# Attention: rope steps of the batch two ahead in the first part of a batch, its norm one batch sooner, the residual on GpSimd

## What is computed

```python
q = _layernorm(x); k = v = ctx_1024                      # (16, 256, 256) -> heads of 16
q = q * cos + rotate_half(q) * sin
k = k * cos + rotate_half(k) * sin
scores = einsum('bqhd,bkhd->bhqk', q, k) / 4 + slope[h] * (key - query)
out = einsum('bhqk,bkhd->bqhd', softmax(scores), v)
x = x + tanh(g_xattn[1]) * out
```

## Time and profile before

| | |
|---|---|
| median of 3 runs | 859.51 us (857.71 to 860.60) |
| profiled execution | 860.34 us, its span 858.2 us |
| mean granted TensorE clock | 0.93 |
| TensorE busy | 713.5 us (83% of the span) |
| VectorE busy | 708.5 us (83%) |
| ScalarE busy | 488.0 us (57%) |
| GpSimd busy | 431.1 us (50%) |
| 256 row maxima, VectorE | 166.3 us, 687 ns each |
| chain that ended last | TensorE 33%, VectorE 30%, issue 16%, GpSimd 9%, ScalarE 8% |

### The profile page before, as it was taken

One profiled execution on the slowest core, in us unless ns is written; L12 is line 12 of the kernel. 1 busy time (PEld: TensorE's weight loads), 2 busy tenths in 40 slices (PEclk: granted clock), 3 DMA queues, 4 the chain that ended last, 5 costly groups with the idle time before them and its releaser, 6 DMA issues.

```text
span 858.2 us, 16571 instructions
## 1 busy us (share of the span) xinstructions
PE 713.5 (83%) x5090; PEld 517.0 (60%) x5090; DVE 708.5 (83%) x1230; ACT 488.0 (57%) x939; POOL 431.1 (50%) x331
## 2 busy tenths in 40 slices
PE   2255999999999998779999999999999775777775
PEld 1255888887888877556565555656565333444444
DVE  6867788998889887868898989898888658888885
ACT  3433545445454342337777777777778674555553
POOL 4524565555655545644444554555443526655553
PEclk8576999999999999879999999999999987888898
DMA  8800000000000000010000000000001000100011
GB/s 279 246 3 0 1 1 1 0 0 0 0 0 1 1 1 1 1 50 2 3 2 2 1 1 1 2 1 1 1 1 50 2 1 1 37 25 24 26 37 50
DMA packets 17719, 18.35 MB, mean 21 GB/s; under 512 B 1670, under 2 KB 16912, under 8 KB 17680
## 3 DMA queue, kind: packets, MB, share of 16 engines
q1 hardware_dynamic: 17084, 17.66, 6.4%
q10 hardware_dynamic: 596, 0.20, 0.1%
HBM read 13.39 MB, written 4.19 MB: 20 GB/s over the span
## 4 chain that ended last, share of the span: by engine, by line
PE 33%; DVE 30%; issue 16%; POOL 9%; ACT 8%; DVEq 1%; DMA 1%; POOLq 1%; ACTq 0%; SPq 0%
PE a_ps_t L561 7%; PE a_ps_m L579 6%; DVE maxima L1497 5%; PE a_ps_pv L615 4%; DVE f_ps_small L1582 4%; PE a_ps_s L600 3%; POOL hs L1110 3%; PE ps_o L522 3%; DVE hup L1324 2%; DVE f_hcode L1598 2%; DVE yup L1293 2%; POOL xres L1090 2%; DVE hscale L1318 2%; ACT hmag L866 1%; PE a_ps_pv L623 1%
## 5 line engine op out<-in xcount | busy, mean ns | idle before, releaser
L1497 DVE TENSOR_REDUCE maxima<-a_ps_m 128x2 f32<-128x512 f32 x256 | 166.3, 687 | 35.4 <-PE a_ps_m L579 34.7
L919 ACT ACTIVATE probs<-a_ps_s 128x512 f32<-128x512 f32 x256 | 149.2, 602 | 42.3 <-PE a_ps_s L600 40.1
L579 PE MATMUL a_ps_m<-stack_t 64*128 64x256 f32 x512 | 107.5, 328 | 19.9 <-DVE maxima L1497 16.7
L579 PEld LDWEIGHTS a_ps_m<-stack_t 64*128 64x128 f32 x512 | 68.3, 188 | 78.7 <-DVE maxima L1497 49.5
L600 PE MATMUL a_ps_s<-stack_t 64*128 64x256 f32 x512 | 100.0, 308 | 3.7 <-ACT probs L919 2.9
L1141 POOL TENSOR_TENSOR stack<-roped,stack 128x512 f32<-128x512 f32 x32 | 42.6, 1333 | 116.8 <-DVE stack L1487 115.3
L491 PE MATMUL ps_gu<-w1h,yth 128*128 128x352 f32 x256 | 88.6, 346 | 13.2 <-DVE h L1311 13.2
L522 PE MATMUL ps_o<-w2t,hqt 128*128 128x256 f32 (+1 forms) x384 | 97.9, 390 | 0.2 <-ACT hqt L851 0.2
L615 PE MATMUL a_ps_pv<-probs,v_aug 128*32 128x256 f32 x1024 | 83.0, 396 | 2.9 <-ACT probs L919 2.5
L910 ACT CAST stack_t<-a_ps_t 128x512 fp32r<-128x512 f32 x128 | 70.9, 588 | 24.5 <-PE a_ps_t L561 23.7
L561 PE MATMUL a_ps_t<-idf,stack 128*128 128x128 f32 x512 | 77.2, 294 | 9.0 <-POOL stack L1141 4.6
(11 more groups left out here) (176 smaller groups left out, 1613.3 us busy)
## 6 DMA issues: line engine op xcount, KB each, us to landing
xres<-in_x SPq DMA_DIRECT2D x16, 256.0 KB, 3.2
ctx<-in_ctx SPq DMA_DIRECT2D x16, 256.0 KB, 3.8
out_x<-f_y SPq DMA_DIRECT2D x16, 256.0 KB, 2.1
w1a_raw<-in_w_gate_up SPq DMA_DIRECT2D x1, 1024.0 KB, 6.2
w_raw<-in_w_fc SPq DMA_DIRECT2D x1, 1024.0 KB, 5.7
w_raw<-in_w_proj SPq DMA_DIRECT2D x1, 1024.0 KB, 5.0
w_raw<-in_w_down SPq DMA_DIRECT2D x1, 704.0 KB, 9.3
stack_t<-neg_max_t SPq DMA_DIRECT2D x32, 8.0 KB
```

Source lines behind the costliest of these rows:

```text
L579: ins = nc.tensor.matmul(a_ps_m[:, half, n, :], a_stack_t[b.par][rows, 0, pair, c * P:(c + 1) * P], a_stack_t[b.par][rows, 1, pair, :], st ...
L919: nc.scalar.activation(a_probs[:, u % 8], a_ps_s[:, u % 2], ACT.Exp).then_inc(a_exp, 1)
L1497: nc.vector.tensor_reduce(a_maxima[:, b.par, c, 4 * quad + half:4 * quad + half + 3:2], a_ps_m[:, half], X, ALU.max).then_inc(a_v_max, 1)
```

## The change

- VectorE, body of a batch b: rope sum and cast of k of b+2, then reciprocals and shares of b-1, rope sum and cast of q of b+2, statistics of b+3; rstd/4 and the two norm steps of b+3 come after m=5. The rope sum and the cast of q leave the places after m=5 and m=8.
- GpSimd, body of b: low parts of k and q of b+2, the residual of b-1 (new here), rstd, k products and q products of b+3.
- The gate is taken into v: ScalarE's copy of v becomes a multiplication by the gate. VectorE's gated residual (L1511) goes; GpSimd adds `a_attn` to `xres` (`at_add`).
- New waits: GpSimd for the shares, VectorE's shares for the residual of the batch before, and in the last layer every batch's statistics for that batch's residual, with a semaphore step of VectorE's own behind the wait.
- Before the loop the second batch's norm comes ahead of the maxima, its rope and cast of k after m=3, those of q after m=5, and the third batch's statistics and norm after m=9 and m=12. `ahead` is 3 in place of 2, so four batches at the end are written out on VectorE and GpSimd in place of two.

```diff
-V_QK = ["stats0", "stats1", "aggr0", "aggr1", "var", "rope_k", "k_hi", "rstd4", "norm0", "norm1", "rope_q", "q_hi"]
+V_QK = ["stats0", "stats1", "aggr0", "aggr1", "var", "rstd4", "norm0", "norm1", "rope_k", "k_hi", "rope_q", "q_hi"]
-G_QK = ["k_cos", "k_sin", "rstd", "k_lo", "q_cos", "q_sin", "q_lo"]
+G_QK = ["rstd", "k_cos", "k_sin", "q_cos", "q_sin", "k_lo", "q_lo"]
-V_OUT = ["recip0", "recip1", "share0", "share1", "add"]
+V_OUT = ["recip0", "recip1", "share0", "share1"]
+ATT_AHEAD = 3
...
-                nc.scalar.copy(a_v_aug[:, b.par, :, :, 0:HD].rearrange("p c h d -> p (c h) d"),
-                               tiles(ctx, b).rearrange("p c (h d) -> p (c h) d", d=HD)).then_inc(a_v, 1)
+                nc.scalar.mul(a_v_aug[:, b.par, :, :, 0:HD].rearrange("p c h d -> p (c h) d"),
+                              tiles(ctx, b).rearrange("p c (h d) -> p (c h) d", d=HD), gates[:, 1:2]).then_inc(a_v, 1)
...
+            def at_add(b):
+                pool.wait_ge(a_v_out, upto(V_OUT, b, "share1"))
+                nc.gpsimd.tensor_tensor(tiles(xres, b), tiles(xres, b), a_attn[:, :, :], ALU.add).then_inc(a_g_add, 1)
+
             def at_body(b):
-                nxt2 = b.shifted(2)
+                nxt2, nxt3 = b.shifted(2), b.shifted(3)
                 if nxt2:
-                    at_k_parts(nxt2)
-                    at_rstd(nxt2)
                     at_low_part(nxt2, 1)
-                    at_q_parts(nxt2)
                     at_low_part(nxt2, 0)
-                elif b.shifted(1):
+                if b.shifted(-1):
+                    at_add(b.shifted(-1))
+                if nxt3:
+                    at_rstd(nxt3)
+                    at_k_parts(nxt3)
+                    at_q_parts(nxt3)
+                if b.shifted(1) and not nxt2:
                     w34_round(0)
                     w34_round(1)
...
-            def at_add_attention(b):
+            def at_share(b):
...
+                if b.shifted(-1):
+                    dve.wait_ge(a_g_add, b.shifted(-1).count(1, 1))
...
-                dve.wait_ge(a_v_out, upto(V_OUT, b, "share1"))
-                nc.vector.scalar_tensor_tensor(tiles(xres, b).rearrange("p c d -> p (c d)"), a_attn[:, :, :].rearrange("p c d -> p (c d)"),
-                                               gates[:, 1:2], tiles(xres, b).rearrange("p c d -> p (c d)"),
-                                               ALU.mult, ALU.add).then_inc(a_v_out, 1)
 
             def at_body(b):
-                nxt2 = b.shifted(2)
+                nxt2, nxt3 = b.shifted(2), b.shifted(3)
                 if nxt2:
-                    at_qk_a(nxt2)
                     at_rope(nxt2, 1)
                     at_high_part(nxt2, 1)
-                    at_qk_norm(nxt2)
-                if b.shifted(-1):
-                    at_add_attention(b.shifted(-1))
+                if b.shifted(-1):
+                    at_share(b.shifted(-1))
+                if nxt2:
+                    at_rope(nxt2, 0)
+                    at_high_part(nxt2, 0)
+                if nxt3:
+                    at_qk_a(nxt3)
...
-                    if nxt2 and m == 5:
-                        at_rope(nxt2, 0)
-                    if nxt2 and m == 8:
-                        at_high_part(nxt2, 0)
+                    if nxt3 and m == 5:
+                        at_qk_norm(nxt3)
 
             def ff_input_stats(b):
                 p = b.par
+                dve.wait_ge(a_g_add, b.count(1, 1))
+                dve.sem_inc(f_alone, 1)
...
             at_lay(1)
             at_qk_a(second)
-            at_rope(second, 1)
-            at_high_part(second, 1)
             at_qk_norm(second)
             for m in range(MU):
                 at_row_max(first, m)
+                if m == 3:
+                    at_rope(second, 1)
+                    at_high_part(second, 1)
                 if m == 5:
                     l0_add_ffn(last)
                     at_rope(second, 0)
-                if m == 8:
                     at_high_part(second, 0)
-            over_batches(dve, at_body)
+                if m == 9:
+                    at_qk_a(third)
+                if m == 12:
+                    at_qk_norm(third)
+            over_batches(dve, at_body, ATT_AHEAD)
...
-            at_add_attention(last)
+            at_share(last)
```

More of the change, by code:

```diff
@@ L335, in build_main @@
         a_alone = sem("a_waits_alone")
+        a_g_add = sem("a_residual_ready")
         f_v_ln, f_g_rstd, f_v_shift, f_a_norm = sem("f_v_ln"), sem("f_rstd_ready"), sem("f_shift_ready"), sem("f_normed")
@@ L1227, in _ @@
             l0_hidden_quantised(last)
+            at_rstd(second)
             at_k_parts(second)
-            at_rstd(second)
+            at_q_parts(second)
             at_low_part(second, 1)
-            at_q_parts(second)
             at_low_part(second, 0)
-            over_batches(pool, at_body)
+            at_rstd(third)
+            at_k_parts(third)
+            at_q_parts(third)
+            over_batches(pool, at_body, ATT_AHEAD)
             for b in lead[:3]:
@@ L1239, in _ @@
             ff_input_up(lead[1])
+            at_add(last)
             ff_input_rstd(lead[4])
```

## The result

The changed kernel takes 874.75 us (median of 6 runs, 871.71 to 875.46) against 860.06 us for the kernel before in the same comparison (857.10 to 861.08). The ratio is 1.0168, 95% interval 1.0144 to 1.0193: 14.7 us slower, where the prediction said 861.6 and its range ended at 868. The profiled execution took 872.27 us with a span of 870.5, so its span is 12.3 us above the 858.2 of before. It is one of the faster of the six runs, 2.5 us under their median.

What follows compares the result with a forecast made beforehand. The prediction took TensorE's order (scores, then P times V) to set the pace nearly everywhere in a batch's second part. Its terms, 1.9 + 0 + 0 - 0.4 + 0.7 - 1.3 + 1.2 = +2.1 us, gave 861.6 us; range 855 to 868.

Steps and rivals of the forecast that it cites:

- item 2: After m=5, rstd4 and norm replace the rope sum: m=6 0.25 us later, +1.9 us over 13 batches (0 to 12.6).
- Item 5: Batch 13, which loses rope and cast and gets no norm: -0.4 us (down to -1.2).
- item 8: Last layer's loop: extra wait and semaphore step before each batch's statistics, 0.15 us for 8 batches: +1.2 us (0 to +2.0).
- Item 1: Cast after m=8 leaves a batch's second part: 0.60 us of VectorE, 0.12 us of the path.
- Items 3 and 4: Rearranged first part of a batch has VectorE slack, and ScalarE has time for v's multiplication by the gate: 0 us each.
- Item 6: Start of the attention stage, with rope, cast, statistics and norm moved: +0.7 us (0 to +1.4).
- Item 7: End of the attention stage: VectorE's residual leaves the chain before the first statistics and after the last shares: -1.3 us (0 to -1.3).
- The rival of a blocked norm: Norm at m=5 waits for GpSimd's second k product, up to 10.7 us over 13 batches: 872 us, 15% chance.
- The rival of VectorE as the bound: VectorE binds the second part, which shortens by 0.35 us for each of 13 batches: 854.3 us, 17% chance.

Runs made afterwards that it cites:

- run 3: Changed kernel plus four more small matmuls per batch on TensorE, queued ahead of the scores for maximum 8 and adding zero: 863.34 us.
- run 4: Kernel before plus a 160-column copy into an unused tile on VectorE, behind the rope sum after maximum 5: 867.43 us.
- run 5: Kernel before plus a 256-column reduction into an unused tile on VectorE, behind the cast after maximum 8: 864.19 us.
- run 10: On top of run 8, norm pair split: rstd4 and first half after maximum 8, second half after maximum 12: 849.71 us.
- run 6: Kernel of run 2 with the residual taken back from GpSimd to VectorE behind the shares: 859.08 us.
- run 7: Kernel of run 2, first batch's maxima: second batch's q rope sum and cast after maximum 4, third batch's statistics after maximum 5: 856.48 us.
- run 8: On top of run 7, last layer's loop without wait and semaphore step ahead of the statistics; one wait before the loop: 853.28 us.
- run 9: Changed kernel with only the last layer's wait and semaphore step ahead of the statistics moved out of the loop: 871.76 us.
- run 1: Changed kernel with the norm pair split: rstd4 and first half after maximum 5, second half after maximum 8: 859.45 us.
- run 2: Changed kernel with the whole norm pair after maximum 8 instead of after maximum 5: 859.75 us.

## Why the prediction was wrong

The step that failed is the second item, and in it what it left out. It followed the 0.25 us through both queues and got +0.13 us per batch at m=9; the batches without a drop measured +0.13 (0.08 to 0.17), and the run with the filled wait gave +1.4 us for the loop where items 2 and 5 together said +1.5 (with one of item 2's 13 batches lying ahead of the loop). So the path was read right at the higher clock. But the same reading says that m=6, and with it TensorE's wait, comes 0.25 us later, 0.95 instead of 0.70, and I priced that wait only by who comes late behind it. The clock of 1.00 went into the sum as a fact about the stage, when it was a condition of it: no rival let it fall, and the 9.2 us lie there. Runs 3 and 4 show it from both sides. With it, +2.1 would have been +11.3, near the 11.9 us between the two profiled executions. The medians are 14.7 us apart; item 8 at the 3 us of the medians would bring the sum to about +13.

The profile of before had a warning that I didn't use: in the stages on both sides of the loop, where TensorE waits more, the granted clock was lower,

```profile
345.00:405.55 60.55, 48.72 (x317) 34.56 (x316) 46.60 (x83) 29.15 (x58) 31.05 (x23) 0.86 0.06 19
659.42:697.86 38.44, 30.91 (x274) 17.08 (x272) 23.04 (x57) 27.67 (x53) 19.07 (x10) 0.91 0.01 2
```

(windows of the kernel before, columns as above), and the loop itself had one wait in each batch that the insertion after m=5 made. Whether 0.25 us more on it would matter couldn't be read from that profile; that it could should have been a rival, with a place and a price.

Point by point:

- Item 1 (0.12 us of path for the cast): consistent with the undisturbed batches. But the price of an insertion after m=8 is not constant. Beyond the cast's 0.60 us every further 0.33 was paid in full (run 5), and 0.37 less of the norm's 0.85 gave 0.34 back (run 10).
- Items 3 and 4 right: the first maximum still waits 1.13 us for the scores, the residual is free in the first part (run 6), and ScalarE's multiply takes 0.71 us, inside the bounds, with no one waiting.
- Item 5: -0.6 against -0.4, right.
- Item 6: +0.7 forecast. From the first maximum to the second batch's it was +2.0, of which at most 0.7 came back before it; so about +1.4, the upper bound. As predicted, the norm met GpSimd's products; the estimate of the waits that it would fill was too kind, and run 7 got 1.55 back by putting the statistics into a wait and the norm behind the products.
- Item 7: -1.3 forecast. From the last shares to the last layer's first output the profile shows -0.5 us; run 6 shows no loss from undoing the move. The first of the two places isn't on the chain that matters, or drops of the clock between the last maximum and the shares (granted 0.74 from 677 to 690 us) hide it; I can't tell which.
- Item 8: right in place. +1.2 forecast; 0.18 us a batch at the higher clock, so +1.5, and about +3 by the medians of runs 8 and 9, beyond its bound of 2.0. The pair of profiles shows only +0.4 over the eight steps (78.6 us against 78.2), with the clock at its lower level for 20.5 us against 23.9 before.
- The rival of a blocked norm was 872, closest to the result, for a reason that didn't occur: the norm ran free.
- The rival of VectorE as the bound was wrong for this change, but the claim against it (TensorE's order sets the pace nearly everywhere) was too strong: with VectorE's insertions placed otherwise the same work runs in 246.36 us instead of 253.87, at the same clock and with TensorE busy for the same 235.4 us.

What stays open: why drops come in every other batch or in runs of batches; whether the length of the one wait decides or the little work around it, which no run here parts; and why the medians give the last layer's wait twice what it shows.

## What to carry to other kernels

When an edit makes another engine's work longer between two groups of matmuls, read the wait that it leaves on TensorE as well as who is late behind it: here 0.15 to 0.25 us more on a wait of 0.70 cost 6 to 9 us by the clock alone. A piece of work of the same length can be harmless a few instructions later, where TensorE has something queued; split it, or put it into a wait that the engine has anyway. And a clock of 1.00 in the profile of before is a state to be defended, not a constant for the sum.

## What the runs showed of the hardware

In the loop of attention, with one wait of 0.85 to 0.98 us per batch of 19.5 us, TensorE's granted clock fell in 6 of 13 batches in the changed kernel and in run 4, and in 7 in run 9. With longest waits of 0.70 to 0.73 (before), 0.65 (run 1), 0.42 (run 3) and 0.38 (run 2) it never fell there, nor with two of 0.73 and 0.45 in the same second part (run 5). All 19 drops began 0.0 to 1.5 us after the end of the long wait. Each lasted 3.4 us (one 6.8), and a batch with one of 3.4 was 1.05 to 1.56 us longer than the same batch before, 0.1 to 0.2 of which the batches without a drop have too. The same wait was followed by a drop in some batches and not in others. The Trainium skill, page "TensorE: Matmul & The Clock Gate", section "HAM oscillation — how this bites in real kernels", has the same back and forth of the clock behind waits for DMA, much longer than these; its next section, "A second HAM failure mode: psum-queue depth-cycling", says that short idle times between groups of matmuls over PSUM banks can do it too, and the trace agrees with that: these are waits for a PSUM half, under 1 us each.

For the port between VectorE and GpSimd, the Trainium skill's page "SBUF — State Buffer", section "Who interferes with whom", says that the two share one pair of ports, and one of them holds it alone. The variance step that moved beside GpSimd's low part took 0.36 us (0.17 in the kernel before), and rstd4 1.11 us beside the products against 0.16 without. The trace agrees with that rule; in the first part of a batch the longer steps lie in slack and cost nothing.
